# Global attention with the score maxima computed one and a half heads ahead instead of two, and the small products, inverses and divisions moved later

## The chip, the core and the metric

The kernel is one program on one core of a Trainium2 chip. The engines that matter here are TensorE (PE, with its weight loads as PEld), VectorE (DVE), ScalarE (ACT), GpSimd (POOL) and SyncE (SP), which only issues DMAs. Each engine works through its own list of instructions in order and waits on semaphores. The metric is the device time of one launch in microseconds (us); lower is better.

## The reference, cut to what matters

A block of adaptive layer norm, global attention with ALiBi and rotary positions, and then two layers of windowed attention with a gated MLP. The change touches the global attention alone:

```python
B, L, D = 2, 1024, 128;  H, KV, HD = 16, 4, 64
q = rope((x @ Wq) as (B, H, L, HD));  k = rope((x @ Wk) as (B, KV, L, HD));  v = (x @ Wv) as (B, KV, L, HD)
k, v = repeat each of the 4 key/value heads for its 4 query heads
attn = q @ k.T / sqrt(HD) + slope[h] * (key position - query position)
attn = softmax(attn, axis=-1)
out = (attn @ v) @ Wo            # all in float32
```

## The kernel before

Batch and head are flattened into 32 heads (`HEADS`), numbered 0 to 31. A head has 1024 queries and 1024 keys, cut into 8 tiles of 128 (`TB`). The work of one head i is a loop over the key tiles k = 0 to 7, and every engine has this loop written out by hand in a function `head(i)`:

- TensorE computes the scores of key tile k against all queries, `qk_step` (L900): four terms (high and low parts of q and k, and a row of query maxima, `QM`), which land in PSUM banks 0 to 3. ScalarE exponentiates them into `E` (L796). TensorE multiplies `E` by V into banks 6 or 7, `pv_step` (L919).
- The softmax needs the maximum of every query row before its scores are made. `max_step(i, k)` on TensorE (L891) makes the plain scores of query tile k in banks 4 and 5, and `max_step` on VectorE (L824) adds the ALiBi row and reduces over the keys, into one column of `M`. TensorE may write banks 4 and 5 again only when VectorE is done with the tile before (L888). The eight columns of a head are turned by a transpose on TensorE, `turn_m` (L898), copied by ScalarE into `mrow` (`take_m`, L777), and written by two DMAs into `QM` (`load_m`, L684), which `qk_step` of that head waits for.
- The row sums of `E` are built by GpSimd (L733, four adds a head, and L737, which joins its sum with VectorE's) and by VectorE (`sum_step`, L834, two adds a head). TensorE sums them over partitions, `denominators` (L937). ScalarE copies the result (`take_denominators`, L765), SP spreads it over 128 partitions (L692), VectorE inverts it (`invert`, L840), SP writes it to memory (L696) and reads it back as a broadcast (L699, `inv_wide`).
- When two heads are complete, VectorE multiplies their rows of the output `OT` by the inverses, in four quarters (`divide`, L848).

The maxima run two heads ahead: in head i, step k, they are those of head i+2, tile k. So 16 maximum steps stand ahead of head 0 (the lead-in), and heads 30 and 31 hold none. In the loop TensorE takes the key tiles in pairs, which this text calls blocks 0 to 3 of a head (key tiles 0 and 1, 2 and 3, and so on): two score steps, a maximum step, two V steps, a maximum step. The two small products, `denominators(i - 1)` and `turn_m(i + 1)`, stand in block 1, between the V steps and the second maximum step.

VectorE in head i: maximum step at every k, `sum_step` at k = 0 (of the head before) and at k = 5, `invert(i - 1)` at k = 6, and in odd heads from 3 on a quarter of the division behind the maximum step of k = 1, 2, 3 and 4. There are 15 such heads; 14 of them, heads 3 to 29, also have maxima. They are called divide heads here.

After the loop TensorE projects the output (L586), the denominators of head 31 are made in between, and a barrier ends the block when the last division is done.

Of the kernel before, what the change touches and what calls it, by code (L numbers as in the profile page):

```python
# [16 lines left out]
TB = N // P  # L17
# [4 lines left out]
HEADS = B * H  # L22
# [70 lines left out]
def adaln_block(nc, x, wq, wk, wv, wo, f_wqkv, f_qs, f_ks, f_wo, f_lg, f_lb, f_w1, f_b1, f_w2, f_b2,  # L93
# [7 lines left out]
    with ExitStack() as whole:  # L101
# [521 lines left out]
        with ExitStack() as ph:  # L623
# [41 lines left out]
            def scores(s):  # L665
                return banks(2 * s, 2)

            def max_bank(i, k):

                return 4 if i >= 2 else (4, 0, 2)[(TB * i + k) % 3]  # L670

# [4 lines left out]
            with nc.Block() as block:  # L676
                @block.sync
                def _(sp):
# [7 lines left out]

                    def spread_inverse(i, s):

                        need(sp, den_taken, i + 1)
                        need(sp, inv_done, i - 1)  # L690
                        for c in range(4):
                            sp.dma_start(den8[32 * c:32 * c + 32, s, :],  # L692
                                         den_sb[32 * c:32 * c + 1, :].rearrange("o (p e) -> o p e", e=TB)).then_inc(den_in, 16)
                        need(sp, inv_done, i + 1)
                        need(sp, inv_in, 16 * (i - 1))
                        sp.dma_start(inv_d[s].rearrange("(p e) -> p e", e=TB), inv8[:, s, :]).then_inc(inv_out, 16)  # L696
                        need(sp, inv_out, 16 * (i + 1))
                        need(sp, o_done, QUARTERS * (i // 2))
                        sp.dma_start(inv_wide[HD * s:HD * s + HD, :], inv_d[s].partition_broadcast(HD)).then_inc(inv_in, 16)  # L699
# [3 lines left out]
                    def head(i):  # L703
# [6 lines left out]
                        if i + 3 < HEADS:  # L710
                            if i + 3 == H:
                                need_landed(sp, 1)
                            load_qa(sp, i + 3, (i + 3) % 4)
                        if i + 1 < HEADS:
                            load_m(i + 1, (i + 1) % 2)
                        if i > 0:
                            spread_inverse(i - 1, (i - 1) % 2)

                    for i in range(HEADS):
                        head(i)  # L720
                    spread_inverse(HEADS - 1, (HEADS - 1) % 2)

# [28 lines left out]
                def _(act):  # L751
# [27 lines left out]
                    def head(i):  # L779
                        for k in range(TB):  # L780
                            if k == 2 and i > 0:
                                take_o(i - 1)
                            if k == 4 and i > 0:
                                take_denominators(i - 1)
                            if k == 4 and i + 1 < HEADS:
                                take_m(i + 1, (i + 1) % 2)
                            need(act, qk_done, TB * i + k + 1)
# [28 lines left out]
                def _(dve):  # L816
                    def max_step(i, s, k):

                        need(dve, max_mm, TB * i + k + 1)
                        if k == 0:  # L820
# [29 lines left out]
                    def head(i):  # L850
                        for k in range(TB):
                            if k == 0 and i > 0:
                                sum_step(i - 1, (i - 1) % 2, 1)
                            if i + 2 < HEADS:
                                max_step(i + 2, i % 2, k)
                            if 1 <= k <= QUARTERS and i % 2 == 1 and i > 1:
                                divide((i - 3) // 2, k - 1)
                            if k == 6 and i > 0:
                                invert(i - 1, (i - 1) % 2)
                            if k == 5:  # L860
                                sum_step(i, i % 2, 0)

                    for i in range(2):
                        for k in range(TB):
                            max_step(i, i, k)
                    need_landed(dve, 1)
                    for i in range(HEADS):
                        head(i)
                    sum_step(HEADS - 1, (HEADS - 1) % 2, 1)

                    invert(HEADS - 1, (HEADS - 1) % 2)
                    for t in range(EARLY):
# [5 lines left out]
                def _(pe):  # L878
                    def max_step(i, k):
# [7 lines left out]

                        need(pe, max_done, TB * i + k - (2 if i < 2 else 0))  # L888
                        for ch in range(2):
# [10 lines left out]
                    def qk_step(i, k):  # L900
# [4 lines left out]
                        if i == 0 and k < 2:  # L905
                            pe.wait_ge(qm_filled, 3)
                            pe.wait_ge(max_done, 2 * TB - 2 + k)
                        keys = slice(k * P, (k + 1) * P)
# [39 lines left out]
                    def head(i):  # L948
                        for k in range(0, TB, 2):
                            qk_step(i, k)  # L950
                            qk_step(i, k + 1)
                            if i + 2 < HEADS:
                                max_step(i + 2, k)
                            if k > 0:
# [3 lines left out]
                            pv_step(i, k)  # L958
                            if k == 2:
                                small_products(i)  # L960
                            if i + 2 < HEADS:
                                max_step(i + 2, k + 1)

                    for i in range(2):
                        for k in range(TB):
                            max_step(i, k)
                            if (i, k) == (1, 2):
                                turn_m(0, 0)
                    for i in range(HEADS):
# [669 lines left out]
```

## Time and profile before

| | |
|---|---|
| median of 3 runs | 1168.59 us (1167.81 to 1170.69) |
| profiled execution | 1173.57 us, of which the recorded span is 1171.8 us |
| TensorE busy | 1083.7 us (92%) |
| VectorE busy | 900.8 us (77%) |
| GpSimd busy | 721.4 us (62%) |
| ScalarE busy | 637.6 us (54%) |
| granted TensorE clock, mean | 0.965 of 2.4 GHz |
| global attention loop, first score product to the end of head 31 | 136.2 to 724.0 us |

Busy time is what the profiler recorded for the engine's own instructions; the end of a matmul is modelled, so a busy TensorE still can have short waits inside. A timeline row gives start, duration, engine, source line, operation, output and input, and in brackets how long the engine stood idle before it and who released it. A head starts at the first `psum<-QH,KH` row of its `qk_step(i, 0)`; head lengths are differences of such starts.

### The profile page before, as it was taken

How to read it: one execution, taken by the hardware profiler on the slowest of the kernel's cores; microseconds unless marked ns; L12 is line 12 of the kernel's file. 1: busy time of each engine (PE TensorE's matmuls, PEld its weight loads, DVE VectorE, ACT ScalarE, POOL GpSimd, SP SyncE). 2: the span in 40 equal slices, each digit the busy share in tenths (PEclk: the TensorE clock that was granted, in tenths of full speed). 3: DMA queues.
4: the chain of work that ended last, by engine and by line, in shares of the span. 5: the costliest groups of instructions: out<-in, count | busy, mean ns of one | idle time of the engine just before them, and what ended most of it. 6: DMA issues, size and time to landing. Idle time of an engine off the chain costs nothing. (4 is left out here: it accounts for less than half of the span.)

```text
span 1171.8 us, 23134 instructions
## 1 busy us (share of the span) xinstructions
PE 1083.7 (92%) x8352; PEld 667.4 (57%) x8352; DVE 900.8 (77%) x1584; ACT 637.6 (54%) x1000; POOL 721.4 (62%) x526
## 2 busy tenths in 40 slices
PE   6882699999999999999999999769999898999988
PEld 4551355554555554554554546736777795777678
DVE  6992767778777788777877765669988588888867
ACT  2442256666566666566666664036666455666554
POOL 3662166666666666657666675699986236666526
PEclk8995699999999999999999999979999999999999
DMA  8899413423434224343243100201111100111111
GB/s 254 276 273 334 96 29 73 106 51 75 81 73 98 59 62 94 74 89 67 57 99 74 38 20 19 91 9 30 33 33 41 25 2 10 38 34 32 33 26 36
DMA packets 83458, 89.03 MB, mean 76 GB/s; under 512 B 32741, under 2 KB 66065, under 8 KB 83345
## 3 DMA queue, kind: packets, MB, share of 16 engines
q1 hardware_dynamic: 83344, 87.55, 29.7%
q8 instruction: 68, 1.11, 0.4%
q14 instruction: 46, 0.37, 0.1%
HBM read 53.57 MB, written 24.25 MB: 66 GB/s over the span
## 5 line engine op out<-in xcount | busy, mean ns | idle before, releaser
L824 DVE CUSTOM_DVE_ANT_0 junk<-psum,alibi 128x1024 bf16<-128x1024 f32 x256 | 312.6, 1221 | 141.8 <-PE psum L891 126.4
L796 ACT ACTIVATE E<-psum,keybias_sb 128x1024 f32<-128x1024 f32 x256 | 275.0, 1113 | 179.1 <-PE psum L915 165.9
L733 POOL TENSOR_TENSOR xpos_sb<-xpos_sb,E 128x1024 f32<-128x1024 f32 x96 | 231.5, 2412 | 127.7 <-ACT E L796 123.3
L927 PE MATMUL psum<-E,V 128*64 128x512 f32 x1024 | 248.0, 605 | 0.0
L891 PE MATMUL psum<-KH,QH 64*128 64x512 f32 x512 | 121.3, 470 | 22.2 <-PEq L275 13.3
L927 PEld LDWEIGHTS psum<-E,V 128*64 128x64 f32 x1024 | 62.1, 136 | 118.0 <-issue 112.0
L737 POOL TENSOR_TENSOR xpos_sb<-xpos_sb 128x1024 f32<-128x1024 f32 x32 | 76.1, 2377 | 68.9 <-DVE xpos_sb L834 68.9
L891 PEld LDWEIGHTS psum<-KH,QH 64*128 64x128 f32 x512 | 49.8, 190 | 116.3 <-DVE M L824 93.4
L915 PE MATMUL psum<-QH,KH 64*128 64x512 f32 x512 | 102.4, 396 | 0.7 <-DVE M L824 0.7
L915 PE MATMUL psum<-QL,KH 64*128 64x512 f32 x512 | 101.5, 392 | 0.0
L915 PE MATMUL psum<-QH,KL 64*128 64x512 f32 x512 | 101.4, 392 | 0.0
L915 PE MATMUL psum<-QM,one_rows 64*128 64x512 f32 x512 | 101.1, 390 | 0.0
L1192 POOL TENSOR_TENSOR rinv_att<-ss_up_att,minus_half 128x16 f32<-128x16 f32 x32 | 93.7, 2928 | 2.7
L733 POOL TENSOR_TENSOR xpos_sb<-E 128x1024 f32<-128x1024 f32 x32 | 76.5, 2391 | 30.3 <-ACT E L796 24.8
L848 DVE TENSOR_TENSOR OT<-OT,XF 128x256 f32<-128x256 f32 x64 | 81.5, 1281 | 3.1 <-DMA XF<-inverse_scratch 3.1
L1316 DVE TENSOR_TENSOR t_att<-psum,xpos_sb 128x512 f32<-128x512 f32 x128 | 79.4, 681 | 5.8 <-PE psum L1396 5.8
L1396 PE MATMUL psum<-fw_qkv,hT_att 128*128 128x512 f32 x128 | 66.9, 649 | 9.1 <-ACT sq_att L1214 6.8
L1286 DVE TENSOR_REDUCE nmax_att<-psum 128x8 fp32r<-128x1024 f32 x32 | 39.1, 1222 | 29.2 <-PE psum L1348 29.2
L915 PEld LDWEIGHTS psum<-QH,KH 64*128 64x128 f32 x512 | 48.5, 186 | 11.6 <-ACT E L796 3.2
L915 PEld LDWEIGHTS psum<-QH,KL 64*128 64x128 f32 x512 | 48.7, 185 | 11.0
L915 PEld LDWEIGHTS psum<-QM,one_rows 64*128 64x128 f32 x512 | 48.5, 185 | 11.1
L1221 ACT ACTIVATE v_att<-psum 128x512 f32<-128x512 f32 x32 | 19.1, 597 | 65.6 <-PE psum L1372 65.6
(145 smaller groups left out, 2096.9 us busy)
## 6 DMA issues: line engine op xcount, KB each, us to landing
QH<-qa_scratch SPq DMA_DIRECT2D x64, 256.0 KB, 4.7
qa_scratch<-tH SPq DMA_DIRECT2D x8, 1024.0 KB, 6.2
qa_scratch<-tL SPq DMA_DIRECT2D x8, 1024.0 KB, 7.8
QL<-qa_scratch SPq DMA_DIRECT2D x64, 128.0 KB, 4.8
XF<-inverse_scratch SPq DMA_DIRECT2D x32, 256.0 KB, 3.6
vp_att<-v_att SPq DMA_DIRECT2D x64, 128.0 KB, 2.3
KH<-k_scratch SPq DMA_DIRECT2D x16, 256.0 KB, 3.9
KL<-k_scratch SPq DMA_DIRECT2D x16, 256.0 KB, 5.2
```

The lines of the kernel that those rows point to most:

```text
L733: pool.tensor_tensor(sum_p[:, s, :], first, E[:, k % 4, :], ALU.add)\
L737: pool.tensor_tensor(sum_p[:, s, :], sum_p[:, s, :], sum_d[:, s, :], ALU.add)\
L796: act.activation(E[:, k % 4, :], scores(k % 2), ACT.Exp, bias=kb).then_inc(exp_done, 1)
L824: dve.tensor_tensor_reduce(junk[:, :], banks(max_bank(i, k), 2), alibi[:, s, :], -1.0, BIG, ALU.add, ALU.min, M[:, s, k:k + 1]).then_inc(m ...
L848: dve.tensor_tensor(o, o, inv_wide[:, cols_], ALU.mult).then_inc(o_done, 1)
L891: last = pe.matmul(banks(max_bank(i, k) + ch), QH[rows, s, k * P:(k + 1) * P], KH[rows, g, ch * 512:(ch + 1) * 512], start=True, stop=True)
L915: last = pe.matmul(scores(k % 2)[:, ch * 512:(ch + 1) * 512], key[rows], query[rows, a:a + 512], start=(n == 0), stop=(n == len(terms) - 1))
L927: last = pe.matmul(banks(6 + i % 2)[HD * ch:HD * ch + HD, :], V[:, g, k, :], E[:, k % 4, ch * 512:(ch + 1) * 512], start=(k == 0), stop=(k ...
L1192: pool.tensor_tensor(rinv[:, s, :], ss_up[:, s, :], minus_half[:, 0:NH], ALU.pow)\
L1286: dve.tensor_reduce(nmax[:, s, :], banks(5, 2).rearrange("p (h c) -> p h c", c=P), AX_X, ALU.max, negate=True).then_inc(max_done, 1)
L1316: dve.tensor_tensor(dst[:, s, n * FH:(n + 1) * FH, :], ps_qk[n], table, ALU.mult).then_inc(done, 1)
L1396: pe.matmul(banks(n), hT[:, t % HR, 0:P], fw_qkv[:, l, n * INNER:(n + 1) * INNER], start=True, stop=True).then_inc(qk_proj, 1)
```

## The change

The lead of the maxima becomes 12 steps (`LEAD`), so that in head i, step k, TensorE and VectorE work on maximum step 8i + k + 12, counted over all heads: tiles 4 to 7 of head i+1 in the first half, tiles 0 to 3 of head i+2 in the second. The lead-in has 12 maximum steps instead of 16, and head 30 now holds four. The small products move from block 1 to block 2 (key tile 4), and there stand ahead of the V steps. On ScalarE `take_m` and `take_denominators` move from k = 4 to k = 6. `invert` is of head i-2 and stands at k = 3, and the divisions come one head later, in even heads from 4 on; the division of heads 28 and 29 and the inverse of head 30 come after the loop. SP's `spread_inverse` is split in two: the spreading of the denominators stays where it was, and the writing and broadcasting of the inverses (`widen_inverse`) comes in the next head, ahead of `load_m`.

```diff
+            LEAD = TB + TB // 2
+            def max_ahead(i, k):
+                return divmod(TB * i + k + LEAD, TB)
             def max_bank(i, k):
-                return 4 if i >= 2 else (4, 0, 2)[(TB * i + k) % 3]
+                return 4 if TB * i + k >= LEAD else (4, 0, 2)[(TB * i + k) % 3]
...
-                    def spread_inverse(i, s):
+                    def spread_denominators(i, s):
                         need(sp, den_taken, i + 1)
                         need(sp, inv_done, i - 1)
                         for c in range(4):
                             sp.dma_start(den8[...], den_sb[...]).then_inc(den_in, 16)
+                    def widen_inverse(i, s):
                         need(sp, inv_done, i + 1)
                         need(sp, inv_in, 16 * (i - 1))
                         sp.dma_start(inv_d[s]..., inv8[:, s, :]).then_inc(inv_out, 16)
                         need(sp, inv_out, 16 * (i + 1))
                         need(sp, o_done, QUARTERS * (i // 2))
                         sp.dma_start(inv_wide[...], ...).then_inc(inv_in, 16)
...
+                        if i > 1:
+                            widen_inverse(i - 2, i % 2)
                         if i + 1 < HEADS:
                             load_m(i + 1, (i + 1) % 2)
                         if i > 0:
-                            spread_inverse(i - 1, (i - 1) % 2)
+                            spread_denominators(i - 1, (i - 1) % 2)
-                    spread_inverse(HEADS - 1, (HEADS - 1) % 2)
+                    widen_inverse(HEADS - 2, HEADS % 2)
+                    spread_denominators(HEADS - 1, (HEADS - 1) % 2)
+                    widen_inverse(HEADS - 1, (HEADS - 1) % 2)
...                      # ScalarE, head(i)
-                            if k == 4 and i > 0:
+                            if k == 6 and i + 1 < HEADS:
+                                take_m(i + 1, (i + 1) % 2)
+                            if k == 6 and i > 0:
                                 take_denominators(i - 1)
-                            if k == 4 and i + 1 < HEADS:
-                                take_m(i + 1, (i + 1) % 2)
...                      # VectorE, head(i)
-                            if i + 2 < HEADS:
-                                max_step(i + 2, i % 2, k)
-                            if 1 <= k <= QUARTERS and i % 2 == 1 and i > 1:
-                                divide((i - 3) // 2, k - 1)
-                            if k == 6 and i > 0:
-                                invert(i - 1, (i - 1) % 2)
+                            if max_ahead(i, k)[0] < HEADS:
+                                max_step(*max_ahead(i, k))
+                            if 1 <= k <= QUARTERS and i % 2 == 0 and i >= 4:
+                                divide((i - 4) // 2, k - 1)
+                            if k == 3 and i > 1:
+                                invert(i - 2, i % 2)
...
-                    for i in range(2):
-                        for k in range(TB):
-                            max_step(i, i, k)
+                    for n in range(LEAD):
+                        max_step(*divmod(n, TB))
...                      # VectorE, after the loop
                     sum_step(HEADS - 1, (HEADS - 1) % 2, 1)
+                    invert(HEADS - 2, HEADS % 2)
+                    for n in range(QUARTERS):
+                        divide(HEADS // 2 - 2, n)
                     invert(HEADS - 1, (HEADS - 1) % 2)
...                      # TensorE, qk_step and head(i)
-                            pe.wait_ge(max_done, 2 * TB - 2 + k)
+                            pe.wait_ge(max_done, LEAD - 1 + k)
...
-                            if i + 2 < HEADS:
-                                max_step(i + 2, k)
+                            if max_ahead(i, k)[0] < HEADS:
+                                max_step(*max_ahead(i, k))
+                            if k == 4:
+                                small_products(i)
                             if k > 0:
                                 pv_step(i, k - 1)
                             elif i > 0:
                                 pv_step(i - 1, TB - 1)
                             pv_step(i, k)
-                            if k == 2:
-                                small_products(i)
-                            if i + 2 < HEADS:
-                                max_step(i + 2, k + 1)
+                            if max_ahead(i, k + 1)[0] < HEADS:
+                                max_step(*max_ahead(i, k + 1))
```

TensorE, end of block 1 and start of block 2 of any head of the middle, before (L891 maximum step, L927 V steps, L937 denominators, L898 turn of the maxima, L915 scores):

```order
L915 MATMUL psum<-QM,one_rows 128x512 x2
L891 MATMUL psum<-KH,QH 128x512 x2
L927 MATMUL psum<-E,V 64x512 x4
L937 MATMUL psum<-xpos_sb,ones_m 32x256 x4
L898 MATMUL psum<-ident,M 8x128
L891 MATMUL psum<-KH,QH 128x512 x2
L915 MATMUL psum<-QH,KH 128x512 x2
```

TensorE in the changed kernel, end of block 2 and start of block 3 (the same operations are L907, L943, L953, L914 and L931 there):

```order
L931 MATMUL psum<-QM,one_rows 128x512 x2
L907 MATMUL psum<-KH,QH 128x512 x2
L953 MATMUL psum<-xpos_sb,ones_m 32x256 x4
L914 MATMUL psum<-ident,M 8x128
L943 MATMUL psum<-E,V 64x512 x4
L907 MATMUL psum<-KH,QH 128x512 x2
L931 MATMUL psum<-QH,KH 128x512 x2
```

The small products moved one block later, and inside the block from behind the V steps to ahead of them.

SP in one head of the middle, behind the loads of the queries, before, with the semaphores that each issue waits for (`QM<-mrow` is `load_m`, `den<-XF` the spreading, `inverse_scratch<-inv` the write and `XF<-inverse_scratch` the broadcast of the inverses, `QL` the last of the query loads):

```order
L164 DMA QL<-qa_scratch 64x512
L684 DMA QM<-mrow 1x4x128 [waits mrow_done,qm_filled]
L684 DMA QM<-mrow 1x4x128
L692 DMA den<-XF 32x1x8 [waits inv_done,den_taken]
L692 DMA den<-XF 32x1x8 x3
L696 DMA inverse_scratch<-inv 128x8 [waits inv_in,inv_done]
L699 DMA XF<-inverse_scratch 64x1024 [waits o_done,inv_out]
```

and in the changed kernel:

```order
L164 DMA QL<-qa_scratch 64x512
L705 DMA inverse_scratch<-inv 128x8 [waits inv_in,inv_done]
L708 DMA XF<-inverse_scratch 64x1024 [waits o_done,inv_out]
L690 DMA QM<-mrow 1x4x128 [waits mrow_done,qm_filled]
L690 DMA QM<-mrow 1x4x128
L698 DMA den<-XF 32x1x8 [waits inv_done,den_taken]
L698 DMA den<-XF 32x1x8 x3
```

The two DMAs of the inverses, with their waits on the inverse and on finished divisions (`o_done`), now stand ahead of the DMAs of the turned maxima.

## Rows read from the trace of the kernel before

**Rows 1.** Stretches, length, busy PE, PEld, DVE, ACT, POOL, clock: heads 3, 28, 29, 30.
```profile
192.44:211.06 18.62, 18.58 (x123) 9.39 (x121) 16.72 (x23) 11.35 (x13) 12.01 (x6) 1.00 0.27 58
653.72:672.02 18.30, 18.30 (x125) 9.39 (x122) 12.07 (x19) 11.36 (x13) 12.07 (x6) 1.00 0.25 59
672.02:690.60 18.58, 18.52 (x124) 9.38 (x121) 16.73 (x23) 10.32 (x12) 11.98 (x6) 1.00 0.07 16
690.60:706.92 16.32, 16.32 (x109) 7.77 (x105) 5.52 (x6) 10.20 (x12) 11.44 (x6) 1.00 0.08 19
```

**Rows 2.** Timeline of TensorE in head 29 (start, duration, engine, operation).
```profile
676.39 0.39 PE L915 MATMUL psum<-QH,KH 64*128 64x512 f32 x2
...
680.42 0.64 PE L937 MATMUL psum<-xpos_sb,ones_m 128*32 128x256 f32 x8
...
681.20 0.50 PE L891 MATMUL psum<-KH,QH 64*128 64x512 f32 x2
681.53 0.40 PE L915 MATMUL psum<-QH,KH 64*128 64x512 f32 x2
...
683.60 0.18 PEld L891 LDWEIGHTS psum<-KH,QH 64*128 64x128 f32 x2 [0.49 <-DVE M L824]
...
684.03 1.94 PE L927 MATMUL psum<-E,V 128*64 128x512 f32 x8
685.90 0.50 PE L891 MATMUL psum<-KH,QH 64*128 64x512 f32 x2
686.23 0.39 PE L915 MATMUL psum<-QH,KH 64*128 64x512 f32 x2
```

**Rows 3.** Timeline of VectorE in head 29.
```profile
677.75 2.13 DVE L848 TENSOR_TENSOR OT<-OT,XF 128x256 f32<-128x256 f32 x1
679.80 1.21 DVE L824 CUSTOM_DVE_ANT_0 junk<-psum,alibi 128x1024 bf16<-128x1024 f32 x1
...
680.95 1.46 DVE L848 TENSOR_TENSOR OT<-OT,XF 128x256 f32<-128x256 f32 x1
682.33 1.21 DVE L824 CUSTOM_DVE_ANT_0 junk<-psum,alibi 128x1024 bf16<-128x1024 f32 x1
...
683.47 0.41 DVE L848 TENSOR_TENSOR OT<-OT,XF 128x256 f32<-128x256 f32 x1
```

**Rows 4.** Timeline of GpSimd in head 29.
```profile
677.22 2.38 POOL L733 TENSOR_TENSOR xpos_sb<-E 128x1024 f32<-128x1024 f32 x1 [0.17 <-POOL xpos_sb L737]
679.75 2.38 POOL L733 TENSOR_TENSOR xpos_sb<-xpos_sb,E 128x1024 f32<-128x1024 f32 x1
683.86 2.38 POOL L733 TENSOR_TENSOR xpos_sb<-xpos_sb,E 128x1024 f32<-128x1024 f32 x1 [1.73 <-ACT E L796]
```

**Rows 5.** Timelines of the lead-in: VectorE, SP and TensorE.
```profile
118.32 1.23 DVE L824 CUSTOM_DVE_ANT_0 junk<-psum,alibi 128x1024 bf16<-128x1024 f32 x1
...
119.70 1.23 DVE L824 CUSTOM_DVE_ANT_0 junk<-psum,alibi 128x1024 bf16<-128x1024 f32 x1
...
129.36 1.41 SPq L684 DMA_DIRECT2D QM<-mrow  x2
...
136.25 0.80 PE L915 MATMUL psum<-QH,KH 64*128 64x512 f32 x2 [0.68 <-DVE M L824]
```

**Rows 6.** A stretch of head 0, columns as in rows 1 (0.62 is the clock).
```profile
139.00:141.00 2.00, 2.00 (x12) 0.91 (x8) 0.07 (x1) 1.47 (x2) 0.00 (x0) 0.62 1.04 213
```

**Rows 7.** Timelines behind the loop: GpSimd, SP, VectorE and TensorE.
```profile
725.22 2.35 POOL L737 TENSOR_TENSOR xpos_sb<-xpos_sb 128x1024 f32<-128x1024 f32 x1 [1.16 <-DVE xpos_sb L834]
...
728.90 2.41 SPq L692 DMA_DIRECT2D den<-XF  x4
...
738.62 1.43 DVE L848 TENSOR_TENSOR OT<-OT,XF 128x256 f32<-128x256 f32 x4 [1.76 <-DMA XF<-inverse_scratch]
...
740.37 1.80 PE L586 MATMUL psum<-wo_sb,OT 128*128 128x128 f32 x14 [1.03 <-PEq L676]
```

**Rows 8.** The broadcast of the inverses, line L699: time from issue to landing.
```profile
DMA to landing us min/median/max: 3.3/3.6/4.5
```

More of the change, by code:

```diff
@@ L816, in _, with max_step @@
                 def _(dve):
-                    def max_step(i, s, k):
+                    def max_step(i, k):
+                        s = i % 2
                         need(dve, max_mm, TB * i + k + 1)
@@ L885, in max_step @@
                             need(pe, mrow_done, 1 if i >= 2 else 0)
-                        need(pe, max_done, TB * i + k - (2 if i < 2 else 0))
+                        need(pe, max_done, TB * i + k - (2 if TB * i + k < LEAD else 0))
                         for ch in range(2):
@@ L958, in head @@
                             pv_step(i, k)
-                            if k == 2:
-                                small_products(i)
-                            if i + 2 < HEADS:
-                                max_step(i + 2, k + 1)
[L964 to L968, printed above, removed]
+                            if max_ahead(i, k + 1)[0] < HEADS:
+                                max_step(*max_ahead(i, k + 1))
+                    for n in range(LEAD):
+                        max_step(*divmod(n, TB))
+                        if n == TB + 2:
+                            turn_m(0, 0)
                     for i in range(HEADS):
```

## The prediction

> **What bounds the kernel now.** I read the shares of the span first (TensorE 92% busy), then the stretches of single heads, then the timelines of one head engine by engine, and last the lead-in and what stands behind the loop. The reader is to see that a head of the middle is TensorE's own pace: head 28 takes 18.30 us and TensorE is busy for all of it at full clock, while VectorE is busy for 12.07 and ScalarE for 11.36 [rows 1]. A divide head is longer: 18.62 us for head 3 and 18.58 us for head 29, the first and the last of 14 (all between 18.57 and 18.63); there VectorE is busy for 16.7 us [rows 1]. The extra 0.3 us is one wait: in block 2 the weight load of the maximum step stands at 683.60 behind 0.49 us of idle time that VectorE ended [rows 2]. Why VectorE is late is in its own rows: a quarter of the division that runs alone takes 0.41 us, but the two before it took 2.13 and 1.46 us [rows 3], and they ended at 679.88 and 682.41, each 0.28 us after an add of GpSimd had ended (679.60 and 682.13) [rows 3, 4]. So in a divide head GpSimd's adds, not the maxima's arrival, set when VectorE is through with the maximum of k = 3: it starts at 682.33 and ends at 683.54, and TensorE goes on at 683.60.
>
> The Trainium skill states the same mechanism (page "SBUF — State Buffer", section on the shared port pair): a VectorE instruction with two SBUF inputs and a GpSimd instruction that reads SBUF lock each other out for a whole instruction, and the one that starts first wins. The rows above agree; the second half of that rule gives the second rival below.
>
> **The lead-in: -4.1 us.** Behind the first steps the maxima come at VectorE's pace, 1.38 us a step (118.32 to 119.70) [rows 5]. Before, the first score product waits for 14 finished steps, and VectorE does end its wait, at 136.25 [rows 5]. Now it waits for 11. Three steps are 4.1 us. What is late next is the row of maxima of head 0: its two DMAs are issued from 129.36 to 130.77 [rows 5], and the new start would be at 132.1, so they have 1.3 us behind the last issue. No row has the landing of this transfer; it moves 2 KB, and if it landed as late as the fastest 256 KB broadcast, 3.3 us after its issue at about 130.1 [rows 8], 1.3 us of the gain would go. I take none. TensorE runs at half clock there and reaches full clock inside 139 to 141 us, some 4 us after the score products begin [rows 6]; I let that point move along with the start. If it stayed at its old time, 4 us more of head 0 would run at 1.2 GHz, at half pace, and give back up to 2 us.
>
> **Four maximum steps into head 30: +1.0 us.** Head 30 has no maxima before and takes 16.32 us against 18.30 [rows 1], so a maximum step costs TensorE 0.25 us in the loop; four are 1.0 us. They are the four that left the lead-in.
>
> **The small products behind the wait: +9.9 us.** Denominators and turned maxima take 0.78 us of TensorE (680.42 to 681.20) [rows 2]; their sum per head does not change by standing elsewhere, so the heads without divisions keep their 18.30 us. In a divide head it matters where they stand. Before, they come ahead of the point at which TensorE meets VectorE (683.60), so they fill time that would be waited. Take the same head with the new order. VectorE's list up to the maximum of k = 3 is the same against the head's start, and so are GpSimd's adds, since what releases them (scores and exponentials of blocks 0 and 1) doesn't move. TensorE reaches the second maximum step of block 1 at 680.42 instead of 681.20, but banks 4 and 5 are free only when VectorE's maximum that began at 679.80 ends, at 681.01 [rows 3]: it waits 0.7 us, and block 2 begins at 681.4 instead of 681.53. Its two score steps are done by 683.3, and the next maximum step waits again until 683.60, as before. Up to here nothing is won. Behind that point before come the V steps (684.03 to 685.90) and block 3 at 686.23 [rows 2]; now the small products stand there too, with no wait left to cover them: +0.78 us. The V steps begin 0.43 us behind the maximum step where the scores elsewhere begin 0.33 behind one [rows 2], so 0.1 us may be absorbed. I take 0.73 us, between 0.68 and 0.78.
>
> The divisions move to even heads. Thirteen of these, 4 to 28, have all their maxima and cost 0.30 + 0.73 = 1.03 us over 18.30, together 13.4. Head 30 has maxima only up to k = 3: it pays the wait in block 1, 0.7 us, and none in block 2. That is 14.1 us against 14 times 0.30 = 4.2 us before: +9.9 us. The inverse (now at k = 3) stands behind the third division, in front of a maximum that TensorE issues no earlier than 683.60, and is hidden there; in the other heads it stands in VectorE's idle time.
>
> **ScalarE's copies** at k = 6 find ScalarE idle, as it is for 7 of 18.3 us [rows 1]: 0. **Behind the loop: +0.6 us.** There the four quarters of heads 28 and 29 are new. GpSimd's last sum runs from 725.22 to 727.57 [rows 7] and locks out the first quarter, which ends 0.28 later, at 727.85; the others run alone, as the last four do, 1.43 us together [rows 7], so they end at 728.9. SP has the broadcast of head 30 waiting for that and the spreading of head 31's denominators queued behind it. The spreading was issued at 728.90 [rows 7]; now the broadcast goes first and takes half a microsecond: 729.5. This chain ends the block (TensorE stands idle for 1.03 us until 740.37, when the last division has ended at 740.05) [rows 7], so its 0.6 us count in full. Between 0 (GpSimd's sum not in the way) and 3 (the broadcast in the way of the small transfers).
>
> **Sum:** -4.1 + 1.0 + 9.9 + 0.6 = +7.4 us. Against the profiled execution, 1173.57 us (span 1171.8), that is 1181.0 us. The median of the runs shown is 4.98 us lower, so I forecast 1176.0 us, with its own range from 1173 to 1178.5 (0.68 to 0.78 in 13 heads, 1.3 or 2 us less from the lead-in, 0 to 3 behind the loop).
>
> **Rival 1, not slower.** VectorE's chain in a divide head is tied to TensorE's maxima after all. When TensorE offers each maximum 0.78 us earlier, the chain is 0.78 us earlier too, and the wait stays at 0.3 us. Then the divide heads cost what they did (13 instead of 14: -0.3), and the sum is -4.1 + 1.0 + 0.6 - 0.3 = -2.8 us: 1165.8 us. For it speaks that before the first division VectorE does wait for TensorE; against it, that two divisions end at a fixed distance behind GpSimd's adds [rows 3, 4]. It decides if GpSimd's first add of a divide head comes later than VectorE's first quarter. Chance 10%.
>
> **Rival 2, the lock goes the other way.** The third quarter starts at 683.47 and GpSimd's next add at 683.86, just as the quarter ends (683.88) [rows 3, 4]. Block 2 now begins 0.1 us earlier, and so do its exponentials; an add that got in ahead would hold the third quarter until some 686.4, the maximum of k = 4 until 687.5, and TensorE, which wants the next maximum step at 686.6, for 1 us more. Thirteen heads make 13 us: 1189 us. Margin 0.2 to 0.3 us; chance 6%. By the skill's rule (same page) whoever issues first keeps the pair, so the margin is all that counts.
>
> **Rival 3, the maxima's row comes late.** In an even head SP issues the broadcast only when the fourth quarter is done. That one stands behind the add of 683.86 to 686.24 [rows 4], so it ends at about 686.5; the broadcast goes out by 687.1, and the two DMAs of `QM` behind it from 687.1 to 688.5 (1.41 us for two) [rows 5]. The next head would start at 690.60 + 0.7 = 691.3. If `QM` lands with the broadcast, 3.3 to 4.5 us after 686.6 [rows 8], that is 689.9 to 691.1, in time; if it needs as long from its own second issue at 687.8, it is 691.1 to 692.3, up to 1.0 late. At 0.5 us in 13 heads: +6.5, 1182.5 us. Chance 10%. The Trainium skill ("DMA: Bandwidth & Descriptors", queues, rings and completion order) says that descriptors of one ring are consumed in order and that a completion mark lands after all earlier writes of that DMA engine, which would put `QM` no earlier than the broadcast; no row here shows it.
>
> **Chances.** The forecast 70%, rival 1 10%, rival 2 6%, rival 3 10%, something else 4%. The range of 1169 to 1183 us holds the forecast, most of rival 3 and part of the rest, and leaves out rivals 1 and 2. A measurement of this kernel can tell 0.3%, 3.5 us, from no change: rival 1 falls within that, so faster has 3%, within 0.3% 13%, slower 84%.
>
> **What would show it.** The first score product at 132.1 us. Heads without divisions still at 18.30; even heads 4 to 28 at 19.3; in them the weight load of the last maximum step of block 1 behind a wait that VectorE ends and that is 0.7 us longer than in the heads without divisions, a second wait in block 2, and the four quarters of the division with the first three at 2.1, 1.5 and 0.4 us as before. Head 30 at 18.0. The first score product of an odd head behind no wait for `QM`. The end of the output projection's pause 0.6 us later against the end of the loop. The forecast is wrong if even heads take 18.6 us (rival 1), 20.3 (rival 2), or if the heads behind them start late (rival 3).

## The result and the profile after

The changed kernel takes 1178.84 us (median of 6 runs, 1177.01 to 1180.99) against 1169.83 us for the kernel before (median of 6). The two medians are 9.0 us apart. The ratio of the comparison is 1.0084, with a 95% interval from 1.0071 to 1.0096: the change makes the kernel slower by 0.84%, some 9.8 us. Forecast were +7.4 us (1.0063) and a time of 1176.0 us. The measured time is inside the range of 1169 to 1183 us and 0.3 us above the narrower one of 1173 to 1178.5.

The profiled executions are 1177.83 us (span 1176.0) and 1173.57 us (span 1171.8), only 4.3 us apart. The shown execution of the kernel before began its lead-in 1.5 us later and spent 3.5 us more behind the attention block (431.4 us against 427.9), in parts that the change doesn't touch; all ten experiments show 427.9 to 430.4 us there. So the two traces are compared from the first maximum step to the barrier behind the loop:

| | before | after | difference | forecast |
|---|---|---|---|---|
| first maximum step to first score product | 20.44 | 16.31 | -4.1 | -4.1 |
| heads 0 to 31 | 587.77 | 601.60 | +13.8 | +10.9 |
| end of the loop to the next projection | 16.35 | 15.90 | -0.4 | +0.6 |
| sum | 624.56 | 633.81 | +9.3 | +7.4 |

In the changed kernel the maximum step is L907 on TensorE and L838 on VectorE, the scores L931, the V steps L943, the denominators L953, the turn L914, the exponential L809, the division L862, GpSimd's adds L746 and L750, the inverse's write L705 and broadcast L708, and the load of `QM` L690. First the stretches of three of its heads, 14 (divisions), 15 and 30; columns are start and end, length, busy time and count of PE, PEld, DVE, ACT and POOL, the clock, DMA share and GB/s.

```profile
393.84:413.31 19.47, 18.63 (x125) 9.44 (x122) 16.59 (x23) 11.22 (x13) 12.03 (x6) 1.00 0.25 55
413.31:431.58 18.27, 18.27 (x123) 9.40 (x121) 12.07 (x19) 11.21 (x13) 12.00 (x6) 1.00 0.25 59
697.18:715.08 17.90, 17.32 (x117) 8.53 (x113) 15.00 (x18) 10.06 (x12) 11.43 (x6) 1.00 0.05 17
```

Against [rows 1], a head without divisions is unchanged, a divide head costs 1.17 us more than it (before 0.30), and VectorE's busy time in it is nearly the same (16.59 us, in head 29 before 16.73). TensorE now has 0.84 us of recorded idle time there (19.47 - 18.63).

TensorE's timeline in head 14, to be read beside [rows 2]; with the rows of its weight loads at the two waits:

```profile
400.40 1.94 PE L943 MATMUL psum<-E,V 128*64 128x512 f32 x8
402.90 0.50 PE L907 MATMUL psum<-KH,QH 64*128 64x512 f32 x2 [0.56 <-DVE M L838]
403.24 0.40 PE L931 MATMUL psum<-QH,KH 64*128 64x512 f32 x2
...
405.51 0.50 PE L907 MATMUL psum<-KH,QH 64*128 64x512 f32 x2 [0.28 <-DVE M L838]
405.95 0.64 PE L953 MATMUL psum<-xpos_sb,ones_m 128*32 128x256 f32 x8
406.52 0.27 PE L914 MATMUL psum<-ident,M 128*8 128x128 f32 x1
406.72 1.94 PE L943 MATMUL psum<-E,V 128*64 128x512 f32 x8
408.59 0.50 PE L907 MATMUL psum<-KH,QH 64*128 64x512 f32 x2
408.92 0.39 PE L931 MATMUL psum<-QH,KH 64*128 64x512 f32 x2
```

```profile
402.90 0.19 PEld L907 LDWEIGHTS psum<-KH,QH 64*128 64x128 f32 x2 [1.45 <-DVE M L838]
405.48 0.21 PEld L907 LDWEIGHTS psum<-KH,QH 64*128 64x128 f32 x2 [0.67 <-issue]
```

The two waits stand where the forecast put them, at the last maximum step of block 1 and the first of block 2. The second ends, by the weight load, 11.64 us into the head (405.48 - 393.84); in head 29 before it ended 11.58 us into it (683.60 - 672.02) [rows 2]. From that weight load to block 3 it is 3.44 us now (405.48 to 408.92) and was 2.63 us (683.60 to 686.23): 0.81 us more, the whole length of the small products (0.77 us, 405.95 to 406.72) and a little over. The wait in block 1 costs nothing by itself: block 2 begins 9.40 us into the head (403.24) and began 9.51 us into head 29 (681.53) [rows 2].

VectorE and GpSimd in the same head, which answer to [rows 3, 4]:

```profile
399.58 2.12 DVE L862 TENSOR_TENSOR OT<-OT,XF 128x256 f32<-128x256 f32 x1
401.63 1.21 DVE L838 CUSTOM_DVE_ANT_0 junk<-psum,alibi 128x1024 bf16<-128x1024 f32 x1
...
402.77 1.45 DVE L862 TENSOR_TENSOR OT<-OT,XF 128x256 f32<-128x256 f32 x1
404.15 1.21 DVE L838 CUSTOM_DVE_ANT_0 junk<-psum,alibi 128x1024 bf16<-128x1024 f32 x1
...
405.29 0.41 DVE L862 TENSOR_TENSOR OT<-OT,XF 128x256 f32<-128x256 f32 x1
```

```profile
399.04 2.39 POOL L746 TENSOR_TENSOR xpos_sb<-E 128x1024 f32<-128x1024 f32 x1 [0.17 <-POOL xpos_sb L750]
401.57 2.37 POOL L746 TENSOR_TENSOR xpos_sb<-xpos_sb,E 128x1024 f32<-128x1024 f32 x1
405.57 2.39 POOL L746 TENSOR_TENSOR xpos_sb<-xpos_sb,E 128x1024 f32<-128x1024 f32 x1 [1.63 <-ACT E L809]
```

The chain has not moved by a hundredth against the start of its head: the maximum of k = 3 ends 11.52 us into it (405.36) and ended 11.52 us into head 29 (683.54). Two quarters again end 0.27 and 0.28 us behind an add of GpSimd.

The lead-in, to be read beside [rows 5]: VectorE's eleventh maximum step, the two DMAs of the first row of maxima, and the first score product with its weight load:

```profile
129.20 1.23 DVE L838 CUSTOM_DVE_ANT_0 junk<-psum,alibi 128x1024 bf16<-128x1024 f32 x1
```

```profile
127.81 1.41 SPq L690 DMA_DIRECT2D QM<-mrow  x2
```

```profile
130.55 0.32 PEld L931 LDWEIGHTS psum<-QH,KH 64*128 64x128 f32 x2 [2.53 <-DMA QM<-mrow]
```

```profile
130.58 0.80 PE L931 MATMUL psum<-QH,KH 64*128 64x512 f32 x2 [2.05 <-DVE M L838]
```

One head is longer by another 1.0 us, head 24 (20.48 us). SP's rows there, and the first score product of head 25:

```profile
594.81 0.34 SPq L705 DMA_DIRECT2D inverse_scratch<-inv  x1
599.87 0.45 SPq L708 DMA_DIRECT2D XF<-inverse_scratch  x1
600.41 1.33 SPq L690 DMA_DIRECT2D QM<-mrow  x2
```

```profile
603.29 0.50 PE L931 MATMUL psum<-QH,KH 64*128 64x512 f32 x2 [0.85 <-DMA QM<-mrow]
```

Head 24 is one of those that load the next keys and values. The write of the inverses is issued behind these loads. In most even heads without such loads (6, 10, 14, 18, 22 and 30) the broadcast goes out 2.4 to 2.5 us after the write's issue, when the fourth quarter of the division has ended; here it goes out 5.1 us after it, and 2.6 us of that are waiting for the write alone to land. The load of `QM`, queued behind the broadcast, comes 0.85 us late. In the other heads with such loads (4, 8, 12, 16 and 20) the broadcast goes out 3.2 to 4.3 us after the write's issue, and only in head 20 does that reach TensorE, by 0.1 us.

### The profile page after: what moved, and what is told of

It is laid out like the page before. It is cut to its first block and busy times, and to the rows that moved or that the text cites. A ratio compares the mean times of both kernels' runs of the same rounds, so it can differ in the third digit from the quotient of the medians.

```text
span 1176.0 us, 23134 instructions
## 1 busy us (share of the span) xinstructions
PE 1076.8 (92%) x8352; PEld 662.6 (56%) x8352; DVE 895.3 (76%) x1584; ACT 632.8 (54%) x1000; POOL 721.9 (61%) x526
## 5 line engine op out<-in xcount | busy, mean ns | idle before, releaser
L838 DVE CUSTOM_DVE_ANT_0 junk<-psum,alibi 128x1024 bf16<-128x1024 f32 x256 | 312.8, 1222 | 162.0 <-PE psum L907 147.5
L809 ACT ACTIVATE E<-psum,keybias_sb 128x1024 f32<-128x1024 f32 x256 | 274.7, 1112 | 247.0 <-PE psum L931 231.5
L746 POOL TENSOR_TENSOR xpos_sb<-xpos_sb,E 128x1024 f32<-128x1024 f32 x96 | 231.5, 2411 | 141.6 <-ACT E L809 137.3
L943 PE MATMUL psum<-E,V 128*64 128x512 f32 x1024 | 248.3, 606 | 0.0
L907 PE MATMUL psum<-KH,QH 64*128 64x512 f32 x512 | 120.1, 464 | 30.1 <-DVE M L838 17.1
L907 PEld LDWEIGHTS psum<-KH,QH 64*128 64x128 f32 x512 | 49.9, 189 | 144.8 <-DVE M L838 93.8
L943 PEld LDWEIGHTS psum<-E,V 128*64 128x64 f32 x1024 | 62.2, 136 | 112.2 <-issue 102.0
L750 POOL TENSOR_TENSOR xpos_sb<-xpos_sb 128x1024 f32<-128x1024 f32 x32 | 76.2, 2383 | 68.8 <-DVE xpos_sb L848 68.8
L931 PE MATMUL psum<-QH,KH 64*128 64x512 f32 x512 | 102.5, 396 | 2.9 <-DVE M L838 2.1
L931 PE MATMUL psum<-QL,KH 64*128 64x512 f32 x512 | 101.6, 393 | 0.0
L931 PE MATMUL psum<-QH,KL 64*128 64x512 f32 x512 | 101.5, 392 | 0.0
L931 PE MATMUL psum<-QM,one_rows 64*128 64x512 f32 x512 | 101.2, 390 | 0.0
L746 POOL TENSOR_TENSOR xpos_sb<-E 128x1024 f32<-128x1024 f32 x32 | 76.5, 2391 | 26.1 <-ACT E L809 20.6
L862 DVE TENSOR_TENSOR OT<-OT,XF 128x256 f32<-128x256 f32 x64 | 77.2, 1214 | 0.7 <-DMA XF<-inverse_scratch 0.7
L1411 PE MATMUL psum<-fw_qkv,hT_att 128*128 128x512 f32 x128 | 63.8, 623 | 9.4 <-ACT sq_att L1229 7.2
L931 PEld LDWEIGHTS psum<-QH,KH 64*128 64x128 f32 x512 | 48.6, 186 | 13.9 <-DMA QM<-mrow 4.8
L931 PEld LDWEIGHTS psum<-QM,one_rows 64*128 64x128 f32 x512 | 48.7, 186 | 11.0
L931 PEld LDWEIGHTS psum<-QH,KL 64*128 64x128 f32 x512 | 48.7, 186 | 10.8
L931 PEld LDWEIGHTS psum<-QL,KH 64*128 64x128 f32 x512 | 48.7, 186 | 10.6
```

The costliest lines, as they stand in the source:

```text
L746: pool.tensor_tensor(sum_p[:, s, :], first, E[:, k % 4, :], ALU.add)\
L750: pool.tensor_tensor(sum_p[:, s, :], sum_p[:, s, :], sum_d[:, s, :], ALU.add)\
L809: act.activation(E[:, k % 4, :], scores(k % 2), ACT.Exp, bias=kb).then_inc(exp_done, 1)
L838: dve.tensor_tensor_reduce(junk[:, :], banks(max_bank(i, k), 2), alibi[:, s, :], -1.0, BIG, ALU.add, ALU.min, M[:, s, k:k + 1]).then_inc(m ...
L862: dve.tensor_tensor(o, o, inv_wide[:, cols_], ALU.mult).then_inc(o_done, 1)
L907: last = pe.matmul(banks(max_bank(i, k) + ch), QH[rows, s, k * P:(k + 1) * P], KH[rows, g, ch * 512:(ch + 1) * 512], start=True, stop=True)
```

## Experiments

Times are medians; the kernel before, run beside them, has 1168.4 to 1168.7 us. Ratios are to it; the changed kernel's is 1.0084 (1.0071 to 1.0096). Head lengths are read from the timelines as above.

**1. Denominators back in block 1.**

```diff
-                        if i > 0:                       # small_products, block 2
-                            denominators(i - 1, (i - 1) % 2)
...
                             pv_step(i, k)
+                            if k == 2 and i > 0:
+                                denominators(i - 1, (i - 1) % 2)
```

> The changed kernel with one edit: the denominators (0.57 us of TensorE) stand again in block 1 behind the V steps, ahead of the second maximum step; the turn of the maxima stays in block 2. Theory (the wait for VectorE at the end of blocks 1 and 2 covers what stands ahead of it, and nothing covers what stands behind): the even heads 4 to 28 go from 19.46 us to 18.9, head 30 from 17.9 to 17.3, heads without divisions stay at 18.3; together -8.0 us against the changed kernel. Rival (a divide head is long because VectorE's own list is full, wherever TensorE's small products stand): 19.46 stays, 0 us. Rival (the whole cost comes from the lead): 0 us.

1173.23 us, ratio 1.0046 (1.0030 to 1.0063). The stretches of heads 14 and 15, with the columns of the first stretches above, as in all that follow:

```profile
391.67:410.57 18.90, 18.64 (x123) 9.42 (x121) 16.58 (x23) 11.22 (x13) 12.03 (x6) 1.00 0.23 57
410.57:428.85 18.28, 18.28 (x124) 9.38 (x121) 12.07 (x19) 11.22 (x13) 11.98 (x6) 1.00 0.25 59
```

The divide heads fall from 19.47 to 18.90, by the 0.57 us of the denominators, and the others don't change: their place is what costs. The whole is 5.6 us less than the changed kernel and not 8.0. Heads 16, 20 and 24 now lose 1.0, 0.75 and 0.5 us, most of it in waits for `QM` (0.87, 0.59 and 0.29 us), whose DMAs keep their time while the head gets shorter. But heads 20 and 24 of the changed kernel already lost 1.1 us of this, so it explains only some 1.2 us of what is missing; head 30, at 17.8 us where 17.3 were expected, is another 0.5 us.

**2. The lead alone back to 16 steps.**

```diff
-            LEAD = TB + TB // 2
+            LEAD = 2 * TB
```

> The changed kernel with a lead of 16 maximum steps again, all else as changed. Theory: the first score product stands 20.4 us behind the first maximum step again instead of 16.3 (+4.1), head 30 goes from 17.9 to 16.3 us (no maxima, -1.6), divide heads stay at 19.46: +2.5 us. Rival (the shorter lead is what makes VectorE late, since its maxima come sooner to be needed): divide heads fall to 18.6, 13 times 0.86, and the sum is -8.7 us.

1183.42 us, ratio 1.0128 (1.0113 to 1.0144), about 5 us slower than the changed kernel. Ten divide heads take 19.35 to 19.39 us (heads 12, 20 and 24 take 19.73, 20.01 and 19.89; the two last end in waits of 0.45 and 0.34 us for `QM`), so the lead is not what makes them long. The lead-in is 21.82 us, 5.5 us longer and not 4.1: the first score product waits for `LEAD - 1` steps, 15 here, where the kernel before waits for 14. I had missed that one step. Head 30 takes 16.33. Trace sum against the changed kernel: +5.5 - 2.6 in the loop + 0.1 = +3.0 us; the profiled executions differ by 5.4 us, and the other 2.4 us lie ahead of the lead-in (0.8) and behind the block (1.6), in parts that the edit doesn't touch.

**3. GpSimd's first two adds narrow** (its sum leaves out key tiles 0 to 2).

```diff
+                            first = E[:, k % 4, :] if n == 2 else first
+                            w = 64 if n < 2 else N
-                            pool.tensor_tensor(sum_p[:, s, :], first, E[:, k % 4, :], ALU.add)
+                            pool.tensor_tensor(sum_p[:, s, 0:w], first[:, 0:w], E[:, k % 4, 0:w], ALU.add)
```

> The changed kernel with the first two of GpSimd's four adds of each head cut to 64 of 1024 columns (the third adds the tile of k = 4 to itself over all columns), so the sum over key tiles 0, 1 and 2 is left out of GpSimd's part. Theory (GpSimd's adds lock VectorE's first two quarters out, and that sets the wait): the quarters take 0.4 us each, VectorE is in time at k = 3, the even heads 4 to 28 take 18.3 to 18.4 us: -15 us against the changed kernel. Rival (VectorE's own work fills the head): the divide heads stay above 19 us, at most -3 us.

1168.19 us, ratio 0.9992 (0.9981 to 1.0003). The stretch of head 14, then its division and GpSimd's adds around it:

```profile
390.34:408.63 18.29, 18.29 (x124) 9.44 (x121) 14.06 (x23) 11.21 (x13) 7.40 (x6) 1.00 0.23 59
```

```profile
396.07 0.42 DVE L864 TENSOR_TENSOR OT<-OT,XF 128x256 f32<-128x256 f32 x1
398.14 0.42 DVE L864 TENSOR_TENSOR OT<-OT,XF 128x256 f32<-128x256 f32 x1
400.44 0.42 DVE L864 TENSOR_TENSOR OT<-OT,XF 128x256 f32<-128x256 f32 x1
402.54 1.06 DVE L864 TENSOR_TENSOR OT<-OT,XF 128x256 f32<-128x256 f32 x1
```

```profile
395.55 0.32 POOL L748 TENSOR_TENSOR xpos_sb<-E 128x64 f32<-128x64 f32 x1 [0.17 <-POOL xpos_sb L752]
397.04 0.32 POOL L748 TENSOR_TENSOR xpos_sb<-xpos_sb,E 128x64 f32<-128x64 f32 x1 [1.17 <-ACT E L811]
401.42 1.89 POOL L748 TENSOR_TENSOR xpos_sb<-E 128x1024 f32<-128x1024 f32 x1 [4.07 <-ACT E L811]
```

With the adds out of the way three quarters take 0.42 us each, the fourth still stands behind an add, and the divide head is as short as any other. VectorE still has every instruction of its list; it is the lock that makes it late. The gain is 10.7 us and not 15: six odd heads now wait for `QM` at their start, the longest 1.45 us, 5.1 us together, so that the even heads ahead of them (4, 8, 12, 16, 20, 24) still take 18.85 to 19.91 us. Experiment 8 takes that away.

**4. The load of `QM` first.**

```diff
-                        if i > 1:
-                            widen_inverse(i - 2, i % 2)
                         if i + 1 < HEADS:
                             load_m(i + 1, (i + 1) % 2)
+                        if i > 1:
+                            widen_inverse(i - 2, i % 2)
```

> The changed kernel with SP's load of the turned maxima ahead of the write and broadcast of the inverses again. Theory (late QM only where the key and value loads are in the way): the waits for QM (0.85 us ahead of head 25, 0.1 to 0.3 in three others) go, all else stays: -1 us, not to be told from 0 in the times. Rival (the broadcast behind the fourth quarter holds up SP and later TensorE in every even head): -0.13 us or more in each of 13 heads, -2 us or more.

1178.61 us, ratio 1.0090 (1.0075 to 1.0105): as expected no difference that can be timed. In the trace the loop is 600.18 us against 601.60, and heads 20 and 24 take 19.45 and 19.46 us. Head 12 stays at 19.75, so its 0.3 us has another cause: its first quarter takes 2.42 us instead of 2.13 and the rest of the chain follows. Why that quarter is late was not found.

**5 and 6. The divisions of the loop on GpSimd**, 5 in the changed kernel (with the edit of experiment 4), 6 in the kernel before.

```diff
                             pool.tensor_tensor(sum_p[:, s, :], first, E[:, k % 4, :], ALU.add)...
+                            if n in (1, 2) and i % 2 == 0 and i >= 4:      # 6: i % 2 == 1 and i > 1
+                                for q in range(2):
+                                    divide(pool, (i - 4) // 2, 2 * (n - 1) + q)
...                      # VectorE
-                            if 1 <= k <= QUARTERS and i % 2 == 0 and i >= 4:
-                                divide((i - 4) // 2, k - 1)
```

> The changed kernel with the four quarters of each division of heads 4 to 30 on GpSimd instead of VectorE (two behind its add of k = 2, two behind its add of k = 4), and SP's load of the turned maxima ahead of the inverses. Theory (a divide head is long only because VectorE's quarters are locked out behind GpSimd's adds; GpSimd itself is idle for about 6 us a head): every head of the middle takes 18.3 us and head 30 17.2, the sum is -15 to -16 us against the changed kernel, which is 7 to 8 us faster than the kernel before. Rival (GpSimd's quarters lock VectorE's sums out or make GpSimd's adds late, so that exponentials wait): even heads stay above 18.8 us, at most -9 us.

> The kernel before with the quarters of each division of heads 3 to 31 on GpSimd in the same places, the lead of 16 and all else as before. Theory: the divide heads 3 to 29 go from 18.6 to 18.3 us, -4 us against the kernel before; it stays 3 us slower than the same edit on the changed kernel, which is what the shorter lead is worth. Rival (the lead is worth nothing once the divisions are out of the way): the two versions take the same time.

Experiment 5: 1161.75 us, ratio 0.9935 (0.9923 to 0.9948). Experiment 6: 1165.67 us, ratio 0.9967 (0.9955 to 0.9980). The stretches of head 14 in experiment 5, of head 15 in experiment 6, and GpSimd's quarters in the first:

```profile
388.22:406.50 18.28, 18.28 (x124) 9.39 (x121) 12.07 (x19) 11.22 (x13) 14.74 (x10) 1.00 0.21 56
```

```profile
410.55:428.85 18.30, 18.30 (x124) 9.38 (x121) 12.30 (x19) 11.34 (x13) 14.78 (x10) 1.00 0.23 59
```

```profile
395.95 2.39 POOL L754 TENSOR_TENSOR xpos_sb<-xpos_sb,E 128x1024 f32<-128x1024 f32 x1
398.29 1.44 POOL L688 TENSOR_TENSOR OT<-OT,XF 128x256 f32<-128x256 f32 x2
399.68 2.39 POOL L754 TENSOR_TENSOR xpos_sb<-xpos_sb,E 128x1024 f32<-128x1024 f32 x1
402.00 1.46 POOL L688 TENSOR_TENSOR OT<-OT,XF 128x256 f32<-128x256 f32 x2
```

A quarter takes GpSimd 0.7 us, and four fit into its idle time: all heads from 1 to 29 take 18.27 to 18.30 us in both kernels. Without a wait in the divide heads it costs nothing where the small products stand, and the shorter lead shows its own worth: 3.9 us between the two medians (in the traces 20.43 - 16.29 = 4.1 us won in the lead-in, 0.8 us given back in the loop, and 0.4 us won behind it, 3.7 us together). The two kernels also differ in the places of the small products and the inverses, which the equal heads of the middle show to be worth nothing here. Experiment 5 beats the kernel before by 0.65%.

**7. Experiments 1 and 4 together.**

> The denominators back in block 1 (as in the first experiment) and SP's load of the turned maxima ahead of the inverses. Theory: the 2.3 us that the first experiment fell short of its -8.0 were waits for QM behind the heads that also load keys and values; without them heads 4 to 28 take 18.9 us each, -8 us against the changed kernel, within 2 us of the kernel before. Rival (they come from something else): heads 16, 20 and 24 stay 0.4 to 1 us longer than the other even heads.

1170.51 us, ratio 1.0014 (1.0004 to 1.0023): -8.3 us against the changed kernel. Heads 16, 20 and 24 take 18.90, 18.89 and 18.91 us and no wait for `QM` is left.

**8. Experiments 3 and 4 together** (the same part of the sums left out).

> GpSimd's first two adds narrow (as in the third experiment, part of the sums left out) and SP's load of the turned maxima ahead of the inverses. Theory: all heads of the middle take 18.3 us, and the six waits for QM (5 us) go: -15 to -16 us against the changed kernel. Rival: the longer heads 4, 8, 12, 16 and the starts of 21 and 25 stay.

1162.30 us, ratio 0.9937 (0.9923 to 0.9951): 5.9 us faster than experiment 3 and as fast as experiment 5. The loop is 584.10 us against 590.53 in experiment 3.

**9. The kernel before with its denominators made twice.**

```diff
-                        for c in range(4):
+                        for c in tuple(range(4)) * 2:
```

> The kernel before with the four denominator products of every head made twice (0.57 us more of TensorE in block 1, ahead of the point where it waits for VectorE's maximum of k = 3 in the divide heads). Theory (work ahead of that point is covered as far as the wait of 0.3 us goes): heads without divisions go from 18.30 to 18.87 us and divide heads from 18.60 also to 18.87, so the divide heads pay 0.27 us instead of 0.57 and the two kinds become equal; together about +13 us. Rival (a divide head is longer by its own amount, whatever TensorE has to do): divide heads at 19.17 us, +18 us.

1178.55 us, ratio 1.0084 (1.0069 to 1.0099), 10 us more than the kernel before beside it, where 13 were expected. Heads 14 and 15:

```profile
398.03:416.74 18.71, 18.71 (x132) 9.62 (x129) 12.07 (x19) 11.35 (x13) 12.27 (x6) 1.00 0.26 58
416.74:435.51 18.77, 18.77 (x133) 9.64 (x130) 17.05 (x23) 11.34 (x13) 12.06 (x6) 1.00 0.24 57
```

The second set costs 0.42 us and not 0.57 where nothing hides it (18.71 against 18.29; TensorE's own rows give 1.01 us for both sets, 406.44 to 407.45), and 0.19 us in divide heads (18.77 against 18.58): 0.23 of the 0.30 us of waiting is filled. In the whole trace the heads without divisions take 18.67 to 18.73 us and the divide heads 18.77 to 18.80, within 0.13 us of each other where they were 0.3 us apart, as the cover would have it, and far from the 19.0 us that the rival would make of it with the measured 0.42.

**10. The small products of the changed kernel behind the V steps of block 2.**

```diff
-                            if k == 4:
-                                small_products(i)
...
                             pv_step(i, k)
+                            if k == 4:
+                                small_products(i)
```

> The changed kernel with both small products behind the V steps of block 2 instead of ahead of them. Theory (only the block matters: both places are behind the wait for the maximum of k = 3): even heads stay at 19.4 to 19.5 us, 0 us. Rival (what hurts is that the V steps come later): even heads back to 18.7, -10 us.

1179.25 us, ratio 1.0087 (1.0070 to 1.0104). Divide heads take 19.44 to 19.50 us (heads 8 and 12: 19.64 and 19.75): the side of the V steps doesn't matter, the block does. Head 30 alone goes from 17.9 to 18.7 us. The first score product behind it waits for `QM`, whose two DMAs go out 15.8 us into head 30 (712.42 - 696.64) where they went out 15.0 us into it (712.22 - 697.18):

```profile
715.34 0.50 PE L931 MATMUL psum<-QH,KH 64*128 64x512 f32 x2 [0.74 <-DMA QM<-mrow]
```

## Why the prediction came out as it did

**Lead-in, -4.1 us: right**, within 0.05 us (20.44 and 16.31). VectorE's eleventh step ends at 130.43 and the first score product follows at 130.58; before, the same gap was 0.14 us (136.11 to 136.25). So the row of maxima of head 0, which I had taken to be in time without a row for it, cost nothing. But that was luck: the profile puts the weight load at 130.55 down to that row, so as it reads, the row came no more than about 0.1 us before it was needed. Its DMAs hang on the first eight steps, not on the lead, so a still shorter lead would have won next to nothing; that was not tried. Head 0 is no longer than before (19.44 against 19.63 us), and the clock's rise came along with the start: the mean granted clock is 0.50 until 135 us, 0.85 in 135 to 136 us and 1.00 in 139 to 141 us now, and was 0.50 until 140 us, 0.74 in 140 to 141 us and 1.00 in the next microsecond: each time it rises 3.7 to 5.5 us behind the first score product, with TensorE busy all the while since then. Experiment 2 (5.5 us for four steps) and experiments 5 and 6 (4.1 us for three) show the same 1.38 us a step.

**Four maximum steps into head 30, +1.0, and its wait of 0.7: right.** It takes 17.90 us, 1.58 us more, where the two terms make 1.7.

**The small products behind the wait: the mechanism right, the size too small.** That GpSimd's adds set VectorE's chain, and the chain TensorE's wait, is shown by experiments 3 and 5; that the place of 0.57 us of matmuls decides over 0.57 us a head, by experiments 1, 7 and 10; that work ahead of the wait is covered as far as it goes, by experiment 9. The term mis-sized is "0.30 + 0.73 = 1.03 us" for a divide head: measured 1.17 (19.47 - 18.30). I had let 0.1 us of the small products be absorbed by the late start of the V steps; nothing was (0.8 us): what follows the maximum step now, the denominators, begins 0.44 us behind it too (405.51 to 405.95). And TensorE's weight load goes on 0.12 us behind the end of VectorE's maximum instead of 0.06 us. In experiment 2 the divide heads are 0.09 us shorter, with the same order; what sets this was not found. Over 13 heads it makes 1.8 us.

**The range worked out too narrow.** The terms that the forecast lists beside its own range (0.68 to 0.78 us in 13 heads, 1.3 or 2 us less from the lead-in, 0 to 3 us behind the loop) add up to about 1175 to 1181 us, not 1173 to 1178.5.

**Rival 3 came true in one head, 24.** The broadcast did hold back `QM`, but not by its own length, as I had reckoned: by the write before it, which the loads of keys and values delay. That is 0.85 us ahead of head 25, and 0.1 us more each in heads 20, 21 and 25, about 1.3 us with what follows. The transfer itself, whose landing no row gave, can now be read: where TensorE waits for it in the loop, it goes on 2.7 to 3.1 us after the first of the two `QM` issues, in head 0, with no broadcast ahead, 2.74 us after it (127.81 to 130.55). So the issue queued behind the broadcast is what made it late; that it also waited for the broadcast to land, nothing here shows. Where heads are shorter the waits are longer: 1.9 us together in experiment 1, 5.1 us in experiment 3. Experiments 4, 7 and 8 remove it by order alone.

**Rival 1 and rival 2 fall.** VectorE's chain stands still against its head; the third quarter still takes 0.41 us and the add that it races, at 405.57, does not get ahead (recorded starts are 0.28 us apart). By the Trainium skill's page "SBUF — State Buffer", section "Who interferes with whom", the one that issues first keeps the pair for its whole instruction, and the trace agrees: the quarter of 405.29 starts first and takes its 0.41 us.

**Behind the loop, +0.6 us: the step right, the sum not.** The broadcast of head 30 does go ahead of the spreading, and the inverse of head 31 comes 0.6 us later against the end of the loop (9.07 against 8.47 us). But the last division could start 3.4 us after the issue of the last broadcast instead of 4.5 us, which more than pays for it. That is luck: 4.5 us was the slowest of the 32 broadcasts in the trace before, whose median is 3.6 [rows 8], and experiments 6 and 9, which keep that order, have 3.70 and 3.85 us there. From the timelines of VectorE, SP and TensorE of the changed kernel, behind the loop:

```profile
733.31 3.53 DVE L862 TENSOR_TENSOR OT<-OT,XF 128x256 f32<-128x256 f32 x4
...
742.90 0.48 SPq L708 DMA_DIRECT2D XF<-inverse_scratch  x1
...
746.33 1.43 DVE L862 TENSOR_TENSOR OT<-OT,XF 128x256 f32<-128x256 f32 x4 [0.70 <-DMA XF<-inverse_scratch]
...
748.08 4.14 PE L586 MATMUL psum<-wo_sb,OT 128*128 128x128 f32 x35 [0.54 <-PEq L682]
```

In sum: +1.8 (divide heads), +1.3 (`QM`), +0.3 (head 12), -1.0 (behind the loop) and -0.3 (heads 0 and 30) lead from the forecast +7.4 to the trace's +9.3, to within 0.2 us.

## What to carry to other kernels

Before moving work on the busiest engine, find the points at which it waits for another engine, and on which side of them the work will stand: work ahead of such a point is free up to the length of the wait (0.23 us of 0.30 in experiment 9), and the same 0.57 us of denominators cost full price behind it, in every divide head (experiment 1). Then ask what sets that point: here it was neither VectorE's own load nor the maxima, but two adds on GpSimd that lock VectorE's two-input multiplies out, and giving these multiplies to the engine that held the lock removed the wait and let the shorter lead pay. And a small transfer that the next stage needs should not be queued behind one that waits for something else.

## What the runs showed of the hardware

The same order of instructions gave the same times to 0.02 us in head after head (eight of the thirteen divide heads of the changed kernel take 19.46 or 19.47 us), so a term of a hundredth of a head can be read from one trace, where the medians need 1 to 2 us. A repeated set of four 256-column products cost 0.42 us where the first set costs 0.57 us, which fits with a part of it being the change from one matmul shape to another; that was not tried by itself. A 4 KB write that lands in 1.4 us took up to 5 us when it was issued behind some 2 MB of loads.
